# Stores that outlive their stages, and one stage for output projection, norm, router and experts

## The reference

```python
# layer 0
xn = layernorm(x)
x = x + splat_attention(xn) + quantized_swiglu(xn)     # 16 heads; two softmaxes, blended
# layer 1
xn = layernorm(x)
a  = hopfield(xn, memory)                              # 3 steps of entmax over 256 memories
h  = xn + latent_attention(rmsnorm(xn, ln1_w))         # 16 heads of 16, causal, @ o_w (256 x 256)
hn = rmsnorm(h, ln2_w)
logits = hn @ router_w + router_b                      # 7 routed experts
p, idx = top_k(sigmoid(logits), 2); w = p / sum(p)
moe = expert(hn, shared) + sum(w[e] * expert(hn, e))   # expert: (silu(x@g) * (x@u) / 8) @ d, 128 wide
out = x + a + h + moe
```

## Time and profile before

| | us |
|---|---|
| median of three executions | 2293.51 (2287.72 to 2294.94) |
| the profiled execution, its own time | 2289.79 |
| its span | 2288.1 |
| PE busy / PEld / DVE / ACT / POOL | 1935.0 / 1388.0 / 1595.0 / 1283.2 / 532.8 |
| PE without a record from 120.0 to 143.8 | 23.8 |
| between the projections' last matmul and the attention's first | 17.8 |
| from the second attention's end to the first expert matmul | 95.9 |

### The profile page before, as it was taken

How to read it: one execution, slowest core, us unless ns; L and a number is a source line. 1 busy time by engine, 2 the same in 40 slices (tenths; PEclk the granted TensorE clock), 3 DMA queues, 4 the chain that set the end, 5 groups by cost and what they waited for, 6 DMA issues and landing times. The chain is left out here.

```text
span 2288.1 us, 31774 instructions
## 1 busy us (share of the span) xinstructions
PE 1935.0 (85%) x10258; PEld 1388.0 (61%) x10258; DVE 1595.0 (70%) x3617; ACT 1283.2 (56%) x2885; POOL 532.8 (23%) x1013
## 2 busy tenths in 40 slices
PE   4958999999999878777878987876694999984898
PEld 3547566656665567666667866665572566643787
DVE  7655677777776258999988799996464677715554
ACT  3422366667666425888866688885340666643111
POOL 1002011111121214444433344442232111120000
PEclk9979699999999899878789977787895999996899
DMA  2570132313320100000000000000133321001000
GB/s 102 182 181 1 36 70 71 66 43 67 71 70 3 63 1 1 1 1 1 1 1 1 1 1 1 1 1 1 39 115 79 65 57 45 13 6 57 1 1 37
DMA packets 39028, 88.80 MB, mean 39 GB/s; under 512 B 10960, under 2 KB 13136, under 8 KB 37840
## 3 DMA queue, kind: packets, MB, share of 16 engines
q1 hardware_dynamic: 38864, 86.78, 14.7%
HBM read 59.09 MB, written 27.26 MB: 38 GB/s over the span
## 5 line engine op out<-in xcount | busy, mean ns | idle before, releaser
L995 DVE TENSOR_REDUCE negmax<-px 128x2 f32<-128x1024 f32 (+1 forms) x480 | 518.4, 1116 | 192.9 <-PE px L917 162.2
L975 ACT ACTIVATE probs<-pss 128x512 f32<-128x512 f32 (+3 forms) x1152 | 491.6, 496 | 238.5 <-PE pss L937 225.0
L937 PE MATMUL pss<-queries,keys 97*128 97x512 f32 (+3 forms) x1152 | 353.5, 385 | 3.7 <-ACT probs L975 3.1
L917 PE MATMUL px<-keys,queries 96*128 96x512 f32 (+3 forms) x1152 | 345.1, 399 | 3.6 <-DVE negmax L995 3.1
L1541 POOL TENSOR_SCALAR rp<-sw,tau 128x256 f32<-128x256 f32 x576 | 271.8, 499 | 79.4 <-DVE st L1688 72.4
L1372 PE MATMUL pt<-ident,sw 128*128 128x128 f32 x768 | 172.6, 372 | 130.4 <-ACT sw L1470 71.4
L1039 POOL TENSOR_SCALAR_AFFINE_SELECT probs<-probs 128x512 f32<-128x512 f32 x192 | 121.8, 635 | 611.0 <-ACT probs L975 611.0
L937 PEld LDWEIGHTS pss<-queries,keys 97*128 97x128 f32 x1152 | 196.4, 193 | 103.2 <-ACT probs L975 54.3
L1443 ACT ACTIVATE ra<-sw,neg 128x256 f32<-128x256 f32 x576 | 243.2, 514 | 1.9 <-DVE neg L1653 1.9
L917 PEld LDWEIGHTS px<-keys,queries 96*128 96x128 f32 x1152 | 211.9, 205 | 50.5 <-DVE negmax L995 32.9
L1387 PE MATMUL pss<-again,sw 128*128 128x256 f32 x1024 | 237.7, 394 | 0.7 <-ACT sw L1463 0.5
(11 more groups left out here) (360 smaller groups left out, 2675.8 us busy)
## 6 DMA issues: line engine op xcount, KB each, us to landing
queries<-rec_q SPq DMA_DIRECT2D x128, 128.0 KB, 3.2
keys<-rec_k SPq DMA_DIRECT2D x96, 128.0 KB, 3.0
queries<-rec_q SPq DMA_DIRECT2D x128, 64.0 KB, 3.1
keys<-rec_k SPq DMA_DIRECT2D x96, 64.0 KB, 3.0
rec_q<-fs SPq DMA_DIRECT2D x16, 256.0 KB, 4.3
rec_k<-fs SPq DMA_DIRECT2D x16, 256.0 KB, 4.7
rec_q<-hi SPq DMA_DIRECT2D x8, 256.0 KB
rec_q<-lo SPq DMA_DIRECT2D x8, 256.0 KB
```

Of the source, the lines that this page charges most:

```text
L917: x = e.matmul(to[:, n, :], ops.qs[p][0:KROW, w + n, t * P:(t + 1) * P], keys[0:KROW, c:c + width], start=not shared, stop=n == bank[-1] i ...
L937: e.matmul(tl.pss[scores % 3][:, 512 - width:512], keys[0:KROW + 1, j * P:(j + 1) * P], ops.qs[p][0:KROW + 1, w, q1 - width:q1], start=Tru ...
L975: e.activation(tl.probs[unit % self.ring][:, w, 512 - width:512], tl.pss[scores % 3][:, 512 - width:512], ACT.Exp).then_inc(self.exp_made, 1)
L995: e.tensor_reduce(tl.negmax[g % 2][:, c // 512, w:w + number, t], self.parts_of(px, width, number), X_AXIS, ALU.max, negate=True).then_inc ...
```

## The change

Three things are rewritten.

1. `QueriesAndKeys` and `LatentProjections` no longer wait for their stores at their end. The waits move to a method `wait_stored` that is called where it first matters: on SP ahead of a load of those records, on the engine that next writes the place that is stored from. To make that safe the tiles that are stored lie elsewhere: `th` and `tl` take the place of the second attention's heads, and in `QueriesAndKeys` four scratch tiles change places with `hi`, `lo`.
2. `AttentionStart` sets all its constants on POOL, between the fourth and the fifth of SwiGLU's sums, and SP loads behind that.
3. `OutputProjection`, `NormalisedTranspose` and `Experts` become one stage, `OutputAndExperts`. One loop over 27 steps u runs all engines: the projection of tile u, the moments of tile u-1, the norm of four tiles in a batch, the turned tile u-9, the logits of tile u-11. POOL copies all 16 tiles of heads ahead, takes over `xs`, the low parts of the expert weights (by expert) and the sums of h into x. In the expert rounds `down` of the last expert of a block is no longer pulled forward.

```diff
+    def wait_stored(self, e):            # QueriesAndKeys, LatentProjections: what stood at the end of sp
@@ SwiGLU.pool
         for n in range(NT):
+            if n == 4:
+                self.start.clear(e)
@@ AttentionStart
+    def clear(self, e):
+        self.records.wait_stored(e)
+        for p in range(t.early):
+            for tile in t.ks[p]:
+                e.memset(f32(tile[:]), 1.0).then_inc(self.made, 1)
+            for w in t.zeros:
+                e.memset(f32(t.qs[p][:, w, :]), 0.0).then_inc(self.made, 1)
@@ LatentProjections
+        parts = [place[:, 512 * n:512 * n + 512].bitcast(F32R) for n in range(8)]
+        self.th, self.tl = parts[:4], parts[4:]
@@ OutputAndExperts.pe
+        turn(0)
+        turn(1)
+        for u in self.steps_before():                          # 27 steps
+            if t + 2 < NT: turn(t + 2)                         # t = u
+            if t < NT: ... products(po <- ot, wo)
+            t = u - self.TURN                                  # 9
+            ... e.wait_ge(self.xn_made, t + 1); if t >= 2: e.wait_ge(self.xl_made, DC * (t - 1))
+            ... e.transpose(pt <- xn)
+            t = u - self.LOGITS                                # 11
+            ... e.wait_ge(self.xs_made, t + 1); products(pl <- xs, rw)
+        e.wait_ge(self.added, NT)
+        e.wait_ge(self.xl_made, DC * NT)
+        e.wait_ge(self.logits_out, NT)
+            if i == 0:
+                e.wait_ge(self.lo_made, 2 * n + 2)
@@ OutputAndExperts.act
+        for u in self.steps_before():
+            if t < NT: ... e.activation(ot <- po)
+            b = u // 4 - 1
+            if 0 <= b < NT // 4 and u % 4 == 2: half_root(...)
+            if 0 <= b < NT // 4 and u % 4 == 3:
+                for t in range(4 * b, 4 * b + 4): e.activation(xn <- h, scale=rms)
+            t = u - self.TURN: ... e.activation(xh <- pt) x DC
+            if u == 20 or u == 22: ... e.activation(hi[:], raw[:], ACT.Copy)
@@ OutputAndExperts.pool
+        for t in range(NT): e.tensor_copy(o[t] <- heads)
+        for t in range(NT):
+            e.wait_ge(self.xl_made, DC * (t + 1))
+            e.tensor_tensor(xs <- xh, xl, ALU.add)
+        e.wait_ge(self.hi_made, 2)
+        for n in range(NE):
+            for lo, raw, hi in ((self.gl, self.g, self.gh), (self.ul, self.u, self.uh)):
+                e.tensor_tensor(lo[:, :, w], raw[:, :, w], f32(hi[:, :, w]), ALU.subtract)
+            if n == 0:
+                for t in range(4): e.tensor_tensor(x[t] <- x[t], h[t], ALU.add)
+        for t in range(4, NT): e.tensor_tensor(x[t] <- x[t], h[t], ALU.add)
```

More of the change, by code:

```diff
@@ L177, in start, with finish @@
             step(e.bn_stats(self.st[:, t, :], x[:, t, :]))
-    def finish(self, e, step, done):
+    def finish(self, e, step, done, count=1):
         st, mean, var, half = self.st, self.mean, self.var, self.half
@@ L737, with __init__ @@
 class AttentionStart(Stage):
[L741 to L753, removed]
-    def sp(self, e):
[L756 to L759, removed]
+    def __init__(self, k, t, records):
+        self.k, self.t, self.records = k, t, records
+        self.made = k.sem("made")
+    def clear(self, e):
+        t = self.t
+        self.records.wait_stored(e)
[4 more added lines that the diff above has]
+                e.memset(f32(t.qs[p][:, w, :]), 0.0).then_inc(self.made, 1)
+    def sp(self, e):
+        t = self.t
+        self.records.wait_stored(e)
+        for p in range(t.early):
+            e.wait_ge(self.made, (p + 1) * (2 + len(t.zeros)))
+            t.load(self.k, e, p)
 class AttentionTiles:
@@ L1849, in sp, with wait_stored @@
                 ops.load(k, e, 0)
+    def wait_stored(self, e):
         for n in range(4):
@@ L2080, in __init__ @@
         self.xh, self.xl = k.xh, k.xl
+        self.heads = k.heads
         with k.scope():
+            self.wo = k.sb("wo", [P, DC, D])
+            self.o = [k.sb("o", [P, D]) for _ in range(NT)]
+            self.ot = [k.sb("ot", [P, DC, P]) for _ in range(4)]
+            self.g, self.u = k.sb("g", [P, DC, NE * P]), k.sb("u", [P, DC, NE * P])
             self.gh, self.gl, self.uh, self.ul = (k.sb(n, [P, DC, NE * P], F32R) for n in ("gh", "gl", "uh", "ul"))
@@ new lines, in sp @@
+    def sp(self, e):
+        k = self.k
+        e.dma_start(self.wo[:], k.ins["lat_o"]).then_inc(self.wo_loaded, 16)
+        for tile, name in ((self.ln2, "ln2_w"), (self.rb, "router_b"), (self.rw, "router_w")):
+            e.dma_start(tile[:], k.ins[name]).then_inc(self.small_loaded, 16)
+        for tile, name in ((self.g, "moe_gate"), (self.u, "moe_up")):
+            e.dma_start(tile[:], k.ins[name]).then_inc(self.loaded, 16)
+        e.dma_start(self.dw[:], k.ins["moe_down"]).then_inc(self.dw_loaded, 16)
@@ L2200, in dve @@
     def dve(self, e):
-        k, step = self.k, Steps(self.steps)
-        self.m.start(e, k.h, step, range(NT))
-        self.m.finish(e, step, self.var_made)
-        step(e.tensor_tensor(self.m.mean[:], self.m.mean[:], self.m.mean[:], ALU.mult))
-        e.wait_ge(self.steps, step.n)
-        e.tensor_tensor(k.rms[:], self.m.mean[:], self.m.var[:], ALU.add).then_inc(self.squares_made, 1)
-        e.wait_ge(self.root_made, 1)
-        step(e.reciprocal(k.rms[:], k.rms[:]))
-        e.wait_ge(self.gh_made, 1)
-        e.tensor_tensor(self.gl[:], self.g[:], f32(self.gh[:]), ALU.subtract).then_inc(self.weights_lo, 1)
-        e.wait_ge(self.uh_made, 1)
-        e.tensor_tensor(self.ul[:], self.u[:], f32(self.uh[:]), ALU.subtract).then_inc(self.weights_lo, 1)
-        e.wait_ge(self.steps, step.n)
-        e.wait_ge(self.weights_lo, 2)
-        self.norm.dve(e)
+        k, step, stats = self.k, Steps(self.steps), Steps(self.stats)
         step(e.memset(self.probs[:], -1.0))
@@ L2245, in dve @@
         for m in range(NB * NE):
-            i, n, b = m // NE, m % NE, m % 2
-            if n == 0:
-                for t in range(4 * i, 4 * i + 4):
-                    e.tensor_tensor(k.x[:, t, :], k.x[:, t, :], k.h[:, t, :], ALU.add).then_inc(self.h_added, 1)
+            b = m % 2
             e.wait_ge(self.silu_made, m + 1)
```

301 lines of the change are left out of this document (153 added, 148 removed).

## The result

The changed kernel took **2233.55 us**, median of 4 runs (2229.76 to 2239.85), where the kernel before, timed beside it, took 2290.61 (2287.61 to 2294.94): a ratio of 0.9751, 95% interval 0.9727 to 0.9776. Its profiled execution took 2233.73 us, its span 2232.0. The direction was right and the size wrong: the sum had come out at 2245.9 on the profiled execution's scale, 12.2 us too high, and the stated range ended at 2235, just above the median.

A forecast was written before the change was run, and what follows sets the result against it. PE, busy 85%, was taken to leave time only at three seams where it idles: 3.1 + 9.4 + 31.4 = 43.9 off 2289.8 gives 2245.9, plus half of 3.7: 2248 us, range 2235 to 2263.

The forecast's parts named there:

- seams 1 and 2: PE idling behind `QueriesAndKeys` and `LatentProjections` while SP waits for stores: gains of 3.1 and 9.4 us.
- the stores only move: Rival: group 0's keys or group 1's load wait behind the stores' traffic, up to 9.4 comes back: 2257; chance 0.06.
- Seam 1's cover: POOL's eight memsets in SwiGLU make its fifth sum some 1.5 us late; they and the later loads cost nothing.
- P(7): Projection of tile 7, last stage: stalled by ACT's root ahead of its copy, a 4.8 us chain, starting at 2051.3.
- Steps 9 to 15: Last stage: each step a loop through PE and ACT's copy, 2.35 us; seven steps plus norms 17.2.
- the low clock behind the stall: Last stage: PE idling in steps 6 to 8 lowers its clock, 1.1 us more a step for two steps.
- The tail: Last stage from step 16: eight steps 10.0, extras on ACT, then 3.9 us through `xs` and the last logits.
- 5.3 us of extras: Tail work on ACT counted on top: small steps and root 1.2, four norms 1.5, two weight copies 2.6.
- The routing: Last logits to first `down`: POOL's subtractions hold ten DVE instructions 0.6 each, costing 6.0 us; 1.3 saved on h sums.
- The rival without a hold: Routing: POOL does not hold DVE, giving back 6.0 and the clock's 1.0: 2241; chance 0.20.
- The clock at the first `down`: Start of the expert rounds: PE waits longer and comes back at the low clock, 1.0 us more.
- The half of 3.7 us: The earlier median lay 3.7 above its profiled execution; half was added, taking 2245.9 to 2248.

The follow-up runs named there:

- copy_ahead: Changed kernel, but in step u ACT copies the turned heads of tile u+1, ahead of that step's `xh`, instead of tile u's: 2228.16 us (2 runs).
- hi_on_pool: Changed kernel, but both fp32r copies of the expert weights go from ACT to POOL, behind its head copies: 2237.75 us (2 runs).
- pool_pause: Changed kernel, but POOL makes the low parts of experts 2 to 7 only after DVE's first `hz`: 2234.59 us (4 runs).
- copy_and_pause: Changed kernel with ACT's head copies one tile ahead and POOL paused from expert 2 until the first `hz`: 2229.72 us, ratio 0.9722 to the kernel before.

## Why the prediction was right or wrong

- **What bounds the kernel, and seams 1 and 2: right.** The waits cost SP 3.1 to 3.4 and 9.4 to 9.5 us wherever they were put back, against 3.1 and 9.4. The stage's start, 12.5 us earlier by forecast, is 13.1 earlier on the average of nine profiles (of before there is one) and 14.3 in the one compared. The keys, the rival "the stores only move", took nothing.
- **Seam 1's cover: right.** POOL's fifth sum came behind its eight memsets at 177.25, 1.8 us later than the seam's shift explains (1.5 forecast). SwiGLU took 0.7 us longer than before (74.6 from its first matmul to the first attention's), but over the thirteen profiles it takes 73.3 to 74.8, so no cost can be read from that. `fl` kept 0.68 us beside the memsets. That bears out what the Trainium skill says (SBUF, "Who interferes with whom"), that an instruction with two SBUF inputs is held only against one of GpSimd's that reads SBUF.
- **P(7): the mechanism was right, the term too big.** From P(0) to P(7) 12.7 were forecast, 10.4 measured. In the chain of 4.8 us I had put the table load behind the wait for DVE. It ran at 2030.43, while ACT waited: 1.3 of the 2.3 us. The stall that stayed (2.8 us from P(6) to P(7)) has the cause given; `copy_ahead` removed it.
- **Steps 9 to 15: right, the clock behind the stall too dear.** From P(7) to P(9) 3.5 forecast, 4.45 measured; from there to the tail 17.2 and 16.1; and 2.3 stood in the sum for the low clock behind the stall: together 2.4 too much. The low clock came, but P(8) took 2.08 us and P(9) 1.51 instead of 1.13: 1.3 in all. And the last step, with no copy behind it, took 1.6. The loop through ACT's copy is the bound: 2.35 forecast, 2.34 read (2046.79 to 2049.13), and 1.73 without it.
- **The tail: the term that was mis-sized most.** Forecast from step 16 to the last logits 19.2, measured 16.8: 2.4 us too much. The term is the 5.3 us of extras (roots, norms, two weight copies). I laid them on top of eight steps of 1.25, 15.3 in all; measured are 12.4, so by that loop they cost 2.4, though the clock was at half in more than half of it; behind these steps 4.3 came where 3.9 stood. In eight steps of 1.25 ACT works only 0.54 each, so it had 5.7 us to take the extras in. `hi_on_pool` measured two of them: 0.8 where 2.6 stood in the sum. A loop over several engines (10.0 forecast) and one engine's whole work (ACT's was 9.92) are two bounds; where they lie close together, as here, the time lies above the larger (12.4) but well under loop and extras added up (15.3). How the 2.4 that are left divide between roots that DVE was late with and the clock was not tested.
- **The routing: mechanism right, size off.** The hold is there, 3.5 us where 6.0 stood. I took nearly the whole of POOL's instruction for each of ten; it is about half, since a DVE instruction comes at any point of it. From the last logits to the first `down` 14.5 were forecast, 12.05 came. The rival without a hold falls with `pool_pause`.
- **The clock at the first `down`: wrong.** 1.0 stood in the sum; eight took 3.45, before 3.46, and the rest of the span 0.1 more. It had been at half clock in the kernel before as well, so there was nothing to add.
- **Together**: -2.3 (P(7)), -2.4 (steps 7 to 15 with their clock), -2.4 (tail), -2.5 (routing), -0.9 (clock at `down`), +0.1 (start): with rounding -10.5 in the last stage, and -1.8 ahead of it. These 1.8 are luck in part: +3.3 at the first seam and +8.3 in the first attention, which other executions did not have, against what the second attention and the stages between lost. Nearly all misses were costs set too high, each by itself "to be safe" within its bounds; the range reached down only to the one rival that took a single cost away.
- **The half of 3.7 us** added for the medians was not needed: the profiled execution after lies 0.2 above its median. That is 2 of the 14 us.

## What to carry to other kernels

Where small extras are put on an engine inside a pipelined loop, compare that engine's whole work with the loop's length and expect something above the larger of the two, not their sum. Two cheap changes of order are worth looking for in such a stage: a copy that feeds the next tile ahead of the work for an older one, and no two-input work on POOL while DVE goes through a chain of short instructions on the path. When single executions differ by 10 us ahead of the place of interest, judge an edit of 3 us from the stage's own start in the trace.

## What the runs showed of the hardware

- The eight matmuls of the first `down` took 1.99 us where PE had idled 0.91 us ahead of them (`copy_and_pause`), and 3.45 where it had idled 3.58 (the changed kernel): the time lost in a wait is not all that it costs.
- A chain of POOL memsets without a pause kept a DVE cast waiting for all that was left of it, 6.15 us instead of 0.23, over the rest of one memset and six whole ones, 0.9 us apart; between POOL's subtractions DVE got its turn after each. The Trainium skill (SBUF, "Who interferes with whom") gives the ports that DVE and GpSimd (POOL) share to the first to issue "for the whole instruction"; for memsets in a row the run shows more than one.
- A POOL cast of 128 x 2048 (one input) takes 1.90 us, as ACT's, not the 2.8 worked out from the head copies, and it holds a two-input DVE instruction until its end (1.42 us instead of 0.17).
- In the first attention the clock came up at about 241 us in the first profile of the changed kernel; the second profile of the same kernel needed 8.4 us more for that attention. That is more than several of the effects measured here.
